# End terms of the scores: stored whole by the projection stage, split into three bf16 parts by GpSimd in the attend stage

## What is computed

```python
q, k, v = proj(Wq, bq), proj(Wk, bk), proj(Wv, bv)
idx = jnp.clip(pos[None, :] - pos[:, None], -MAX_REL, MAX_REL) + MAX_REL
attn1 = jnp.einsum('bhqd,bhkd->bhqk', q, k)
attn2 = jnp.einsum('bhqd,qkd->bhqk', q, rel_k[idx])
attn = jax.nn.softmax((attn1 + attn2) / scale, axis=-1)
```

## Time and profile before

| what | value |
|---|---|
| median of three runs | 1385.82 us (1384.87 to 1387.82) |
| the profiled execution, its own time | 1384.85 us |
| span of the profiled execution | 1383.1 us |
| mean granted clock of TensorE | 0.972 of full speed |
| busy: TensorE / VectorE / ScalarE / GpSimd | 91% / 69% / 55% / 40% |

### The profile page before, as it was taken

One profiled execution on the slowest core, in us unless ns is written; L12 is line 12 of the kernel. 1 busy time (PEld: TensorE's weight loads), 2 busy tenths in 40 slices (PEclk: granted clock), 3 DMA queues, 4 the chain that ended last, 5 costly groups with the idle time before them and its releaser, 6 DMA issues. The chain is left out here.

```text
span 1383.1 us, 67607 instructions
## 1 busy us (share of the span) xinstructions
PE 1264.9 (91%) x30680; PEld 937.8 (68%) x30688; DVE 955.0 (69%) x1844; ACT 757.8 (55%) x1413; POOL 551.3 (40%) x983
## 2 busy tenths in 40 slices
PE   4387669999999999999999999999999999979998
PEld 3254437777777777777777777777777777756766
DVE  6499876776766767677767676676777776146664
ACT  4367525565655656555656566565666565623332
POOL 4376623443435343434344343534344443122221
PEclk9789959999999999999999999999999999989999
DMA  4544520111020112011111101111211110113231
GB/s 126 141 168 167 179 60 7 42 33 55 23 55 23 52 32 57 21 54 42 33 49 29 55 20 54 30 47 32 56 35 41 45 32 9 41 41 92 69 92 46
DMA packets 101541, 79.08 MB, mean 57 GB/s; under 512 B 13256, under 2 KB 97032, under 8 KB 101256
## 3 DMA queue, kind: packets, MB, share of 16 engines
q1 hardware_dynamic: 101256, 74.77, 18.3%
HBM read 45.90 MB, written 27.26 MB: 53 GB/s over the span
## 5 line engine op out<-in xcount | busy, mean ns | idle before, releaser
L1043 DVE TENSOR_REDUCE b_mx<-b_a 128x1 f32<-128x512 f32 x1024 | 658.7, 685 | 234.0 <-PE b_a L810 228.7
L1004 ACT ACTIVATE b_p<-b_s 128x512 f32<-128x512 f32 x1024 | 569.8, 595 | 399.3 <-PE b_s L851 313.6
L901 PE MATMUL b_pv<-b_p,vg 128*16 128x128 f32 x8192 | 286.7, 275 | 0.1
L774 POOL TENSOR_TENSOR qd<-q,one 48x512 bf16<-48x512 bf16 x256 | 266.2, 1040 | 28.7 <-POOLq L286 3.8
L751 POOL TENSOR_TENSOR b_np<-vg,one 128x16 bf16<-128x16 f32 x192 | 39.1, 264 | 560.7 <-DVE b_mx L1043 550.4
L851 PE MATMUL b_s<-qd,z 112*128 112x32 bf16 (+1 forms) x6016 | 248.8, 189 | 0.7 <-issue 0.6
L810 PE MATMUL b_a<-k,q 48*128 48x512 bf16 x1024 | 202.8, 393 | 26.8 <-DVE b_mx L1043 11.3
L851 PEld LDWEIGHTS b_s<-qd,z 112*128 112x128 bf16 x6016 | 205.8, 99 | 11.0 <-issue 1.0
L901 PEld LDWEIGHTS b_pv<-b_p,vg 128*16 128x16 f32 x8192 | 196.2, 96 | 21.4 <-issue 0.6
L836 PE MATMUL b_s<-q,k 54*128 54x64 bf16 (+3 forms) x4608 | 188.2, 201 | 6.4 <-issue 2.5
L836 PEld LDWEIGHTS b_s<-q,k 54*128 54x128 bf16 (+1 forms) x4608 | 126.4, 95 | 92.4 <-PE b_s L836 29.2
(11 more groups left out here) (125 smaller groups left out, 1321.8 us busy)
## 6 DMA issues: line engine op xcount, KB each, us to landing
x<-in_x SPq DMA_DIRECT2D x32, 256.0 KB, 3.2
scratch_qop<-a_parts SPq DMA_DIRECT2D x16, 384.0 KB, 2.5
scratch_kop<-a_parts SPq DMA_DIRECT2D x16, 384.0 KB, 3.2
k<-scratch_kop SPq DMA_DIRECT2D x32, 192.0 KB
q<-scratch_qop SPq DMA_DIRECT2D x32, 192.0 KB
scratch_v<-a_vr SPq DMA_DIRECT2D x16, 256.0 KB, 3.2
k<-scratch_kop SPq DMA_DIRECT2D x32, 128.0 KB
q<-scratch_qop SPq DMA_DIRECT2D x32, 128.0 KB
```

Source lines behind the costliest of these rows:

```text
L774: nc.gpsimd.tensor_tensor(dst, src, one, ALU.mult).then_inc(s["qd_ready"], 1)
L901: nc.tensor.matmul(PV[32 * a:32 * a + V16, g * P:(g + 1) * P], v[:, 0 if t <= i else 1, t, h, :], PR[at.c % 2][:, t, h, :], start=(t == 0 ...
L1004: nc.scalar.activation(out, src, ACT.Exp, scale=SCALE).then_inc(s["p_ready"], 1)
L1043: nc.vector.tensor_reduce(MX[v.c % 2][:, h:h + 1], PA[(n + hp) % NBANK][:, :], AX_X, ALU.max, negate=True).then_inc(s["a_used"], 1)
```

## The change

The projection stage copies the 64 end terms from PSUM straight into the guard tensor (one instruction in place of five), and the guard tensor has 128 floats for each partition in place of 256. In attend GpSimd splits them once a batch, in four instructions ahead of guard_parts of the batch's first unit; its wait for the batch's guard tensor now stands ahead of the wait for the maxima. The copies into b_np read the bf16 parts.

```diff
-VGW = VW + 4 * T * H
+VGW = VW + 2 * T * H
...
-                        pe.wait_ge(s["dsplit"], at.count())
+                        pe.wait_ge(s["devac"], at.count())
...
                 dve.wait_ge(s["ends"], at.count(1, 1))
-                link(nc.vector.tensor_copy(db[:, 0, :], pd[:, :]))
-                nc.vector.tensor_tensor(dr[:, :], pd[:, :], db[:, 0, :], ALU.subtract).then_inc(s["dsplit"], 1)
+                nc.vector.tensor_copy(GD[p][:, T * H:], pd[:, :]).then_inc(s["devac"], 1)
+                if at.since(1):
+                    dve.wait_ge(s["vdone"], at.count())
                 maxima(0)
-                dve.wait_ge(s["dsplit"], at.count(1, 1))
-                link(nc.vector.tensor_copy(db[:, 1, :], dr[:, :]))
-                link(nc.vector.tensor_tensor(db[:, 2, :], dr[:, :], db[:, 1, :], ALU.subtract))
-                nc.vector.tensor_copy(GD[p][:, T * H:], db[:, :, :].rearrange("p c n -> p (c n)"))
                 maxima(1)
...
+            def end_parts(at):
...
+                pool.wait_ge(v_in[p], (at.even(T) + 1) * 32)
+                nc.gpsimd.tensor_tensor(DB[p][:, 0, :], pd, one, ALU.mult).then_inc(s["ends"], 1)
+                pool.wait_ge(s["ends"], batch * NEND + 1)
+                nc.gpsimd.tensor_tensor(DR[:, :], pd, DB[p][:, 0, :], ALU.subtract)
+                nc.gpsimd.tensor_tensor(DB[p][:, 1, :], pd, DB[p][:, 0, :], ALU.subtract).then_inc(s["ends"], 1)
+                pool.wait_ge(s["ends"], batch * NEND + 2)
+                nc.gpsimd.tensor_tensor(DB[p][:, 2, :], DR[:, :], DB[p][:, 1, :], ALU.subtract).then_inc(s["ends"], 1)
+
             def guard_parts(at):
 
                 p, i = (at.c // T) % 2, at.c % T
+                if i == 0:
+                    end_parts(at)
...
                 pool.wait_ge(s["a_used"], HP * (place[at.count(), HH - 1] + 1))
                 if i == 0:
-                    pool.wait_ge(v_in[p], (at.even(T) + 1) * 32)
+                    pool.wait_ge(s["ends"], (at.it * 2 + at.c // T + 1) * NEND)
...
                 for c in range(3):
-                    e = VW + (T + c * T + i) * H
-                    nc.gpsimd.tensor_tensor(np_[:, 3 + c], heads(VG[p][:, e:e + H]), one, ALU.mult)
+                    nc.gpsimd.tensor_tensor(np_[:, 3 + c], heads(DB[p][:, c, i * H:(i + 1) * H]), one, ALU.mult)
```

More of the change, by code:

```diff
@@ L251, in stage_project @@
     qr = m.sb("a_qr", [P, S])
-    db, dr = m.sb("a_db", [P, 3, T * H], BF16), m.sb("a_dr", [P, T * H])
     gr = m.sb("a_gr", [P, T, H])
@@ L259, in stage_project @@
     names = ("blank", "late", "zeroed", "lv", "var", "eps", "rstd", "shift", "xn", "xT", "xTs", "proj", "qevac", "kevac",
-             "kless", "kpart", "qsplit", "ksplit", "vevac", "ends", "dsplit", "rel", "relmax", "vdone", "dv", "stats", "pl")
+             "kless", "kpart", "qsplit", "ksplit", "vevac", "ends", "devac", "rel", "relmax", "vdone", "stats", "pl")
     s = {n: m.sem("a_s_" + n) for n in names}
     out = k["stored"]
-    NLINK = 3
     z, slot = m.sb("a_z", [P, ZLO_W + ZHI_W]), m.sb("a_slot", [P, PARTS])
@@ L537, in constants @@
                         nc.vector.memset(k["vg"][p][:, 0:VW].rearrange("p (n c) -> p n c", c=V16)[:, :, HD:HD + 1], 1.0)
[L539 to L546, removed]
             def statistics(at):
@@ L567, in step @@
                 p = at.c % 2
-                link = linker(at, 0)
                 def maxima(t):
@@ L609, in stage_attend @@
     MT = m.sb("b_mt", [6 * H, P], BF16)
+    DB = [m.sb(f"b_db{p}", [P, 3, T * H], BF16) for p in range(2)]
+    DR = m.sb("b_dr", [P, T * H])
     idb = m.sb("b_idb", [P, P], BF16)
@@ L616, in stage_attend @@
              "mp_ready", "mt_ready", "mt_copied", "xtt_ready", "norm", "m_in",
-             "qd_ready", "v_ready", "guard")
+             "qd_ready", "v_ready", "guard", "ends")
     s = {n: m.sem("b_s_" + n) for n in names}
@@ L622, in stage_attend @@
     NGD = 3
+    NEND = 3
     NSR = 2 * SUB
@@ L732, in _ @@
         def _(pool):
+            def end_parts(at):
+                p = (at.c // T) % 2
+                batch = at.it * 2 + at.c // T
+                pd = VG[p][:, VW + T * H:VW + 2 * T * H]
+                one = k["one"][:, 0:1].to_broadcast([P, T * H])
+                pool.wait_ge(v_in[p], (at.even(T) + 1) * 32)
[5 more added lines that the diff above has]
+                nc.gpsimd.tensor_tensor(DB[p][:, 2, :], DR[:, :], DB[p][:, 1, :], ALU.subtract).then_inc(s["ends"], 1)
             def guard_parts(at):
                 p, i = (at.c // T) % 2, at.c % T
+                if i == 0:
+                    end_parts(at)
                 def link(n, ins):
```

## The result

| | before | after |
|---|---|---|
| median, four runs of each | 1386.28 us | 1368.56 us (1364.50 to 1370.31) |
| profiled execution, its own time | 1384.85 us | 1367.64 us |
| its span | 1383.1 us | 1365.9 us |
| mean granted clock | 0.972 | 0.973 |

The ratio is 0.9868, with a 95% interval of 0.9842 to 0.9893: 17.7 us faster, between 14.8 and 21.9. The change was run a second time, beside the last experiments and on another chip: 1365.42 us against 1386.79, ratio 0.9846 [0.9828, 0.9865], 21.4 us. Both 95% intervals hold the forecast gain of 20.9 us, and both medians lie in the range of 1360.5 to 1373.

The account below looks back on a forecast made before the run. VectorE's work, partly standing still until GpSimd finished, was taken to bound the projection stage. Gains of 16.7 (steps), 3.3 (before the stall) and 0.9 us (stage's end) sum to 20.9: 1365.0 us, own range 1362 to 1368, overall 1360.5 to 1373.

Parts of the forecast that it names:

- The removed work: Projection stage: a step loses the rest, middle part, low part and widening on VectorE, by medians 2.6 us.
- The new interval: Projection steps: copies of rows come 6.46 us apart by ScalarE's and TensorE's chain; taken as 6.5 us, bounds 6.46 and 6.9.
- The steps with clears and long constants: Projection steps 3 and 4 (GpSimd clears) and 8 and 9 (VectorE constants): 1.0 us together, bounds 0 and 3.
- Before the stall: Early projection stage: step 1's guard store moves from 38.62 to 35.3, gaining 3.3 us, bounds 0 and 3.4.
- The second loop of the prediction: Projection, through the DMA: statistics, two maxima, clamp, guard store, load of rows, landing, statistics again; 6.24 us.
- The end: Last projection step, where three maxima follow the removed instructions and set the stage's end: 0.9 us gained.
- Attend: GpSimd's four added instructions cost about 1.5 us a batch, hidden in its wait for VectorE's maxima; guard tensor already landed.
- Rival B: Projection stage: stretches at 1.2 GHz stay and 4 to 5 us come back, 1369.5 us; chance 0.21.
- Rival C: Projection stage: the clamp waits for a GpSimd split each step, intervals of 7.4 us, 1373 us; chance 0.08.
- D: Projection stage: VectorE was the only bound, intervals fall to 5.6 us, 1353 us; chance 0.06.
- E: Projection stage: no change, the freed time is all waited for elsewhere, 1385.8 us; chance 0.04.
- F: Projection stage: slower, TensorE stays at 1.2 GHz through the stage, 1421 us; chance 0.03.

Follow-up runs that it names:

- the fourfold split: The kernel with the change, with twelve more 128x64 instructions on GpSimd in each batch's split in attend: 1370.11 us, ratio 0.9868.
- the four variants with quicker steps: The change plus earlier row loads, GpSimd's clears in halves, both, or both with step 1's load also earlier: 1369.37, 1369.72, 1368.15, 1367.81 us.

## Why the prediction was right, point by point

**What bounded the kernel: right.** TensorE's waits for the maxima, 16 us outside of the stall, are gone to 1.2 us, and the stage is shorter by what follows from that. That VectorE stood still beside GpSimd is shown by the pair out of SBUF and out of PSUM; that this alone was most of the price is not. Three idle instructions out of SBUF cost 8.3 us, and the three real ones, moved behind the statistics and mostly no longer held up, gained nothing or some 4 us. The change took away both the standing still and the work, and the work counts in steps with long constants.

**The removed work: right.** Between the fourth and the last copy of rows VectorE's busy time fell from 86.76 to 59.00 us, 2.5 us a step for 2.6 forecast, and the interval by 1.4, since something else was late next.

**The copy costed at nothing, with a bound of 1.0 us: right.** It took 225 ns in every step. The source decides, as was taken from the earlier trace rows.

**The new interval: right, and shown.** 6.46 us was worked out from one step; the clean steps take 6.42 or 6.43 in every variant but one, and that one, with one more activation on ScalarE (0.49 us long, some 0.4 from start to start), takes 6.80. That the pace is ScalarE's and TensorE's loop rests on this and on the maximum done twice.

**The steps with clears and long constants: mis-sized.** They were given 1.0 us together (bounds 0 and 3). Ten intervals after the first took 67.7 us where 66.0 were forecast, 1.7 more; over ten clean ones of 6.43 the excess is 3.4 us. What was left out is SyncE's order: stores wait for GpSimd, and the guard store and the load of rows queue behind them. The landing was given some tenths, and in the longest step it took 0.8 us more. The step of 78.04, on rows above, shows both, and with the clears spread the intervals fell to 6.43. Of the eleven intervals, four lie in the 6.4 to 6.6 us that the prediction named as its sign.

**Before the stall: mis-sized.** 3.3 us were forecast; in one profiled execution it was 2.3, in the other 66.80 - 63.08 = 3.7. The second is luck in part: its first copy of rows was at 23.73, 0.9 us before that of the kernel before, and no row shows why. The two first intervals were 6.43 as reckoned. The second loop of the prediction, given 6.24 us, takes 7.24 here, from the statistics at 26.10 to those at 33.34: the guard store is at 29.31, the load 0.75 behind it at 30.06 where it had been 0.37, and the landing takes 3.3. So the statistics of step 1 are 2.04 us behind their copy of rows, not 1.2; with a first copy 0.24 later (24.87) that is the miss of 1.0.

**The end: right.** 0.9 us forecast, 1.0 measured.

**Attend: right in time, wrong in one reason.** "So it has landed" failed: GpSimd waits 68.3 us for the guard tensor, in 14 batches. It costs nothing because the wait lies inside the one that was there, for the maxima. That 1.5 us a batch (1.22 measured) are hidden is shown by the fourfold split. That attend would be the same within 1 us held in the first profile. It is no sharp sign, since over the variants attend lasts 1048 to 1055 us with the same code.

**Rival B, the clock: not in the change, but real.** The stretches at 1.2 GHz of the earlier trace rows are in neither of its profiles. They came back, once each, in the four variants with quicker steps and in the one with three instructions out of PSUM, after TensorE had stood still for 1.6 to 2.9 us behind a late guard store; the stop and the clock together cost 2.2 to 4.8 us, the dearest of them about the price that the rival had.

**Rival C, the clamp: did not occur in the change** (median 196 ns); with the three instructions moved behind the statistics it did. It leaned on the Trainium skill (SBUF — State Buffer, Who interferes with whom), which says that a VectorE instruction in a two-port mode and one of GpSimd exclude each other for the whole instruction, and that a VectorE instruction with at most one SBUF input outside these modes does not contend with GpSimd. The traces agree with both: the clamp took 0.910 us in the median and 1.16 beside GpSimd's split, and the 48 instructions with a PSUM source never took more than 0.283. **D** is excluded by the maximum done twice, **E** and **F** by the time.

**The sum.** The span fell by 17.2 us where 20.9 were forecast, 3.7 less: 1.5 in the steps, 1.0 before the stall, and 1.3 in attend and the output stage, whose code is the same but for the split, less 0.1 at the end. The second profile, with a span of 1362.7, fell by 20.4.

## What to carry to other kernels

Here two small VectorE instructions had medians five times their minima, and both were held up by another engine. Where a profile shows such a gap, look at what runs on GpSimd at the start of the instruction, and whether its operands lie in SBUF or in PSUM. To let three such instructions read PSUM was 5 us cheaper here. To move three of them gained nothing: the wait went to the next instruction of that kind and to TensorE, so ask where every other one then falls, and who waits for the end of VectorE's row. When the bound of a loop goes, count the loops again through the in-order DMA queue, with everything that stands ahead of the load in it. Look also for stretches at a lowered clock behind long stops of TensorE. They are not certain: a stop of 2.40 us had one behind it, a stop of 2.36 us in the kernel with the split behind the statistics had none in the 11 us after it.

## What the runs showed of the hardware that was not expected

- A stop of TensorE can cost more than its own length: a guard store that landed 4.6 us after its issue stopped TensorE for 2.40 us, and 6.8 us at 1.2 GHz followed; the two intervals were 4.3 us too long. A clean step has a wait of 0.65 us at this place, so by estimate some 1.8 us are the stop's and 2.5 the clock's.
- Landing time depends on what is in flight. The load of rows lands 2.7 to 3.1 us after its issue in the kernel before, 2.8 to 3.7 in the change, and 3.7 to 3.8 where it is issued right behind the stores, ahead of the guard store; in the long steps of three variants it took 4.6 to 5.2.
- Three idle VectorE instructions of 0.2 us cost 3.1 us over 16 steps out of PSUM (with one late guard store in the profile) and 8.3 us out of SBUF.
